# A transformer block on one Trainium2 core: the first attention with its queries turned by DMA and its scores in 2-byte parts

## The reference, cut to what matters

```python
def _L0_xattn_ref(text, features, Wq_w, Wq_b, Wk_w, Wk_b, fn_w, qn_w, kn_w):
    features_n = rmsnorm(features, fn_w)
    Q = einsum('btd,fd->btf', text, Wq_w) + Wq_b
    K = einsum('bsd,fd->bsf', features_n, Wk_w) + Wk_b
    Q = rmsnorm(Q, qn_w)
    K = rmsnorm(K, kn_w)
    scores = einsum('btf,bsf->bts', Q, K) / sqrt(512)
    attn = softmax(scores, axis=-1)
    return einsum('bts,bsf->btf', attn, features_n)
x = x + _L0_xattn_ref(_layernorm(x), ctx_4096, ...)
x = x + _L0_ffn_ref(_layernorm(x), ...)       # sparse feed-forward, inner width 1792
x = x + _L1_xattn_ref(_layernorm(x), ...)     # 32 heads over 8 key heads
x = x + _L1_ffn_ref(_layernorm(x), ...)       # 512 x 512 with a row selection
```

## Time and profile before

| | us |
|---|---|
| median of 3 runs (lowest, highest) | 1484.04 (1482.01, 1485.4) |
| the profiled execution, its own time | 1483.17 |
| its span, first to last instruction | 1481.4 |
| PE busy | 1455.0 (98%) |
| DVE busy | 1120.7 (76%) |
| ACT busy | 792.4 (53%) |
| POOL busy | 713.1 (48%) |
| DMA: moved | 150.04 MB, mean 101 GB/s |

### The profile page before, as it was taken

How to read it: one execution, slowest core, us unless ns; L and a number is a source line. 1 busy time by engine, 2 the same in 40 slices (tenths; PEclk the granted TensorE clock), 3 DMA queues, 4 the chain that set the end, 5 groups by cost and what they waited for, 6 DMA issues and landing times.

```text
span 1481.4 us, 27790 instructions
## 1 busy us (share of the span) xinstructions
PE 1455.0 (98%) x9944; PEld 851.6 (57%) x9944; DVE 1120.7 (76%) x2159; ACT 792.4 (53%) x3201; POOL 713.1 (48%) x672
## 2 busy tenths in 40 slices
PE   8999999999999989999999999999999999999998
PEld 7888645555555455556555555655555565555554
DVE  6887787888876878676776776777677677677868
ACT  6678731211223775565556646654754664565663
POOL 6678885554555354343333434333442433343554
PEclk9999999999999999999999999999999999999999
DMA  5844345444343585534443543444454345233543
GB/s 194 245 143 144 121 93 118 100 85 98 70 82 69 124 164 91 132 84 73 102 93 65 106 77 79 98 89 83 89 90 93 81 82 108 53 63 68 105 70 125
DMA packets 363722, 150.04 MB, mean 101 GB/s; under 512 B 346704, under 2 KB 347344, under 8 KB 360640
## 3 DMA queue, kind: packets, MB, share of 16 engines
q1 hardware_dynamic: 362288, 140.92, 44.4%
q10 hardware_dynamic: 1296, 7.34, 1.5%
HBM read 60.11 MB, written 4.19 MB: 43 GB/s over the span
## 4 chain that ended last, share of the span: by engine, by line
PE 59%; DVE 3%; POOL 1%; ACT 1%; issue 1%; SPq 1%; DMA 0%; POOLq 0%; DVEq 0%; ACTq 0%
PE bank L72 19%; PE bank L74 19%; PE bank L73 19%; PE bank L2667 3%; DVE x_res L2343 1%; ACT a_prob L1986 1%; DVE a_oT_lo L2256 0%; POOL a_xr_lo L1863 0%; DVE a_kn L2211 0%; SPq L1735 0%; DVE a_qve L2195 0%; DVE a_p_lo L2244 0%; POOL w L1902 0%; SPq L1731 0%; ACT xln L124 0%
## 5 line engine op out<-in xcount | busy, mean ns | idle before, releaser
L1986 ACT ACTIVATE a_prob<-a_prob,a_nmx 128x64 f32<-128x64 f32 x512 | 170.2, 334 | 247.7 <-DVE a_nmx L2232 247.7
L1838 POOL TENSOR_TENSOR a_prob<-a_prob,a_mask 128x512 f32<-128x512 f32 x64 | 79.8, 1268 | 271.8 <-DVE a_prob L2226 271.8
L72 PE MATMUL bank<-w,xT_hi 128*128 128x448 f16 (+1 forms) x512 | 187.5, 366 | 1.1 <-PEq L1043 1.1
L74 PE MATMUL bank<-w,xT_hi 128*128 128x448 f16 (+1 forms) x512 | 187.3, 366 | 0.0
L73 PE MATMUL bank<-w,xT_lo 128*128 128x448 f16 (+1 forms) x512 | 187.2, 366 | 0.0
L1856 POOL TENSOR_TENSOR a_qrs<-a_qve,neg_half 128x8 f32<-128x8 f32 x64 | 105.0, 1642 | 138.3 <-DVE a_qve L2195 138.0
L2179 DVE SCALAR_TENSOR_TENSOR x_res<-bank,a_oinv,x_res 128x512 f32<-128x512 f32 x128 | 95.6, 747 | 79.4 <-PE bank L74 79.4
L1251 ACT CAST f_h_hi<-h 128x448 f16<-128x448 f32 x64 | 35.6, 563 | 207.2 <-DVE h L1325 207.2
L2184 DVE SCALAR_TENSOR_TENSOR a_qr_lo<-bank,a_qr_hi 128x512 f16<-128x512 f32 x128 | 87.9, 687 | 45.7 <-ACT a_oT_lo L1963 27.3
L1844 POOL TENSOR_TENSOR a_p_hi<-a_prob,a_rden 128x512 f16<-128x512 f32 x64 | 69.4, 1085 | 104.6 <-DVE a_rden L2240 104.6
L1189 POOL TENSOR_TENSOR f_h_lo<-h,f_h_hi 128x448 f16<-128x448 f32 x64 | 72.7, 1140 | 89.0 <-ACT f_h_hi L1251 89.0
(11 more groups left out here) (357 smaller groups left out, 4443.5 us busy)
## 6 DMA issues: line engine op xcount, KB each, us to landing
shared<-in_l_wq SPq DMA_DIRECT2D x8, 1024.0 KB, 4.9
shared<-in_l_wo SPq DMA_DIRECT2D x8, 1024.0 KB, 5.1
shared<-in_w ACTq DMA_DIRECT2D x8, 896.0 KB, 4.6
craw<-in_w SPq DMA_DIRECT2D x11, 512.0 KB, 3.8
a_wide<-in_l_ctxT SPq DMA_DIRECT2D x16, 256.0 KB, 3.9
x_res<-in_x SPq DMA_DIRECT2D x16, 256.0 KB, 4.5
shared<-in_ctx SPq DMA_DIRECT2D x16, 256.0 KB, 4.3
shared<-in_l_wkv SPq DMA_DIRECT2D x8, 512.0 KB, 3.7
```

Of the source, the lines that this page charges most:

```text
L72: pe.matmul(out, a_hi, b_hi, start=first, stop=False)
L74: return pe.matmul(out, a_hi, b_lo, start=False, stop=last)
L1838: pool.tensor_tensor(blocks(prob[u][:, :]), blocks(prob[u][:, :]), mask[:, :].unsqueeze(1).broadcast_to([P, NB, S]), ALU.add).then_inc(s_m ...
L1986: ins = act.activation(pt, pt, ACT.Exp, bias=nmx[:, col:col + 1], accum_out=den[:, col:col + 1])
```

## The change

Six things change, all in the first attention but for the last:

1. The queries stay unturned in their bank. A 13th matmul adds the bias there (`share`, a matrix of 1/64, times the bias rows split in two parts). DVE no longer adds it. `q_bank(n)` alternates between two banks; the one for PE's turned queries is gone.
2. ACT reads the bank, multiplies by the inverse root of the queries and rounds to f16 (`q_hi`), DVE makes the f16 rest (`q_lo`), and SP turns both parts with a DMA transpose each (`queries_T`, 128 x 512 in 2 bytes).
3. Keys are scaled by a power of two and split in f16; the scores are 12 matmuls of f16.
4. The probabilities of tile n-1 are turned, and the values of n-1 multiplied, in body n, behind the keys and the queries of n+1. On PE the scores and the turn of the keys end the body.
5. ACT, DVE, POOL and the start have new orders, shown below. The queue of SP has two transposes in each round, behind the loads and at n = 4 behind the six small loads, too. The w2 loads 2 to 4 of the next stage come behind the last transposes.
6. In the tail, the first product of the next stage (`hidden(0, 0)`) moves ahead of the last `attend`.

```diff
+    part = lambda n: big[:, 4 * KD * D + n * D:4 * KD * D + (n + 1) * D].rearrange("p (k f) -> p k f", k=KD)
+    xT_hi, xT_lo, cT_hi, cT_lo, bq_parts = (part(n) for n in range(5))
+    qT_hi, qT_lo, kT_hi, kT_lo = (turned[:, n, :, :] for n in range(4))
...
+        def queries_T(n):
+            if n:
+                sp.wait_ge(s_s, n)
+            sp.wait_ge(s_qh, n + 1)
+            sp.dma_start_transpose(qT_hi, qr_hi).then_inc(s_qT, 16)
+            sp.wait_ge(s_ql, n + 1)
+            sp.dma_start_transpose(qT_lo, qr_lo).then_inc(s_qT, 16)
...
+            if n >= 4:
+                queries_T(n - 3)
...
+        first_w2()
+        for n in range(NT - 3, NT):
+            queries_T(n)
@@ pool_steps, body @@
             if first:
                 key_root(1)
+                weigh(1)
             tile_roots(n)
+            if project:
+                features_lo(n + 1)
             if ahead:
                 features_T(n + 2)
-            if first:
-                weigh(1)
...
-            if project:
-                features_lo(n + 1)
             if ahead:
                 weigh(n + 2)
@@ act_steps @@
         def first_body():
+            key_squares(1)
+            features_T(2)
+            features(1)
             normalise(2)
-            key_squares(1)
-            squares_c(2)
-            features_T(2)
-            rows_T(2)
-            k_T(1)
-            exps(0)
-            q_T(1)
-            probs_T(0)
-            query_squares(1)
-            features(1)
+            query_squares(1)
+            rows_T(2)
+            squares_c(2)
+            squares_c(3)
...
+        def q_hi(n):
+            wait_query_root(act, n)
+            if n:
+                act.wait_ge(s_qT, 32 * n)
+            act.activation(qr_hi, q_bank(n)[:, :], ACT.Copy, scale=qrs(n)).then_inc(s_qh, 1)
@@ act_steps, body @@
+            k_T(n)
+            exps(n - 1)
+            q_hi(n)
...
+            if ahead:
+                features_T(n + 2)
+            probs_T(n - 1)
+            if project:
                 key_squares(n + 1)
...
+            act.activation(kT_hi, blk(bkT), ACT.Copy, scale=k_up[:, :]).then_inc(s_kTh, 1)
@@ dve_steps @@
-        def query_bias(n):
-            dve.wait_ge(s_q, n + 1)
-            dve.tensor_tensor(qb[:, :], bq_bank[:, :], bq, ALU.add).then_inc(s_qb, 1)
+        def key_scale():
+            dve.tensor_reduce(k_max[:, :], wqk, AX.X, ALU.max, apply_absolute_value=True).then_inc(wqk_ok, 1)
...
+        def q_lo(n):
+            dve.wait_ge(s_qh, n + 1)
+            dve.scalar_tensor_tensor(qr_lo, q_bank(n)[:, :], qrs(n), qr_hi, ALU.mult, ALU.subtract).then_inc(s_ql, 1)
@@ pe_steps, project_q @@
+            pe.matmul(blk(q_bank(n)), share[:, :], bq_parts, start=False, stop=True).then_inc(s_q, 1)
@@ pe_steps, body @@
             if project and not first:
                 project_k(n + 1)
+            if not first:
+                probs_T(n - 1)
+            if project:
                 project_q(n + 1)
-            pe.wait_ge(s_kTl, n + 1)
             if not first:
+                attend(n - 1)
             if ahead:
                 rows_T(n + 2)
...
+            scores(n)
+            if project:
+                k_T(n + 1)
...
+        def scores(n):
+            pe.wait_ge(s_kTl, n + 1)
+            pe.wait_ge(s_qT, 32 * (n + 1))
@@ pe_steps, tail @@
         def last(n):
+            filler(pe, 2)
+            probs_T(n)
+            filler(pe, 3)
             attend(n)
-            filler(pe, 2)
+            filler(pe, 4)
```

More of the change, by code:

```diff
@@ L211, in l0_attention @@
     wide = sb("wide", [P, 7 * D])
-    xn, cw, kn, qb, kb = (wide[:, n * D:(n + 1) * D] for n in range(5))
+    xn, cw, kn, q_rows, kb = (wide[:, n * D:(n + 1) * D] for n in range(5))
+    qr_hi, qr_lo = (q_rows.bitcast(F16)[:, n * D:(n + 1) * D] for n in range(2))
     cT_raw = [wide[:, n * D:(n + 1) * D].rearrange("p (k f) -> p k f", k=KD) for n in (5, 6)]
@@ L223, in l0_attention @@
     css = lambda n: first_ss[:, n:n + 1] if n < 2 else sums[:, 2:3]
-    qss = sums[:, 3:4]
+    first_qss, first_qrs, share = sb("first_qss", [P, 1]), sb("first_qrs", [P, 1]), sb("share", [P, P], F32R)
+    share_f = kb[:, 0:P]
+    k_max, k_pow, k_inv, k_up, s_down = (sb(n, [P, 1]) for n in ("k_max", "k_pow", "k_inv", "k_up", "s_down"))
+    qss = lambda n: sums[:, 3:4] if n else first_qss[:, :]
     rs = lambda n: first_rs[:, n:n + 1] if n < 3 else root4[:, (n - 3) % RING, 0:1]
@@ L851, in split_wq @@
                 dve.tensor_tensor(w_lo[0][:, k, :], w_raw[0][:, k, :], w_hi[0][:, k, :], ALU.subtract).then_inc(wl_ok, 1)
+        dve.wait_ge(half_ok, 3)
+        dve.tensor_copy(share[:, :], share_f).then_inc(off_ok, 1)
         split_wk((0, 1))
@@ L868, in dve_steps @@
         scale_keys(0)
-        q_T(0)
+        key_scale()
+        rows_T(1)
+        q_lo(0)
+        k_T(0)
         statistics(2)
-        k_T(0).then_inc(s_kTl, 1)
-        rows_T(1)
         run(body)(dve)
+        denominators(NT - 1)
+        probs_T(NT - 1)
         before_last()
@@ L979, in pe_steps @@
         pe.wait_ge(half_ok, 2)
-        project_k(0, first=True)
+        project_k(0, first=True, ks=range(0, 2))
         stay_busy(8)
+        project_k(0, first=True, ks=range(2, 3))
         rows_T(0)
-        stay_busy(10)
+        project_k(0, first=True, ks=range(3, KD))
+        stay_busy(6)
         project_q(0, first=True)
```

321 lines of the change are left out of this document (172 added, 149 removed).

## The result

The changed kernel takes 1503.58 us, the median of four runs (1500.62 to 1505.87), against 1483.94 (1482.01 to 1485.40, four runs). The ratio is 1.0128, with a 95% interval of 1.0114 to 1.0142: 1.3% slower. I had said 1491, and 1479 to 1499 as the range, so the sign was right and the size was not.

What follows compares the result with a forecast made beforehand. PE was taken as busy nearly throughout, with a loop through POOL and DVE next to bind. Start +6.7, body 1 +1.1, bodies 2 to 14 -2.4 and tail +2.6 gave +8.0 us, so 1491, range 1479 to 1499.

Steps and rivals of the forecast that it cites:

- Bounds and sign: Whole kernel: the first attention's end shifts the rest one for one; PE saves 0.8 us a body, almost all lost; slower.
- the sum: Whole kernel: +6.7 + 1.1 - 2.4 + 2.6 = +8.0 us on the profiled 1483.17, giving 1491.2.
- The start, +6.7: Up to tile 2's keys: a chain through ACT, POOL and DVE makes them 6.7 us late, bounds 5 to 8.
- Body 1 and SP's queue, +1.1: Body 1: tile 1's transposes queue on SP behind loads and six small loads, adding 1.1 us, bounds 0 to 3.
- Bodies 2 to 14, -2.4: Bodies 2 to 14 of the first attention: 120.3 us against 122.7, so 2.4 us gained.
- The ring: Bodies 2 to 14: a dependency loop through POOL and DVE, including the search, sets most bodies; 9.7 us in 8 to 12.
- 13.6 us of POOL's waiting: Kernel before, bodies 2 to 14: POOL's idle time for the keys' scaling, read as a loop turning at nearly PE's pace.
- The tail, +2.6: End of the first attention, to the first block score: 2.6 us lost to waits and clock, bounds 1 to 5.
- my 0.9 for it: Tail: the slowed PE clock after longer idling costs 0.9 us, beside 1.75 for waits.
- Behind the attention, 0: Everything after the first attention: merely shifted with its end, no term of its own in the sum.
- The clock: Start and body 1: three longer PE waits would each cost another 1 to 1.75 us by the rule, giving 1496.
- Transposes land late in every body: Rival for the bodies: transposes behind loads on SP cost 0.7 us in each of 13, 9 more, 1500; chance 0.12.

Runs made afterwards that it cites:

- e13: Changed kernel with the w1 pieces searched in the order 2, 3, 0, 1, so that two w1 loads fall away; 1500.86 us.
- e9: Changed kernel in which POOL no longer waits for DVE's scaling of the keys ahead of weigh; 1500.04 us.
- e1: Changed kernel in which POOL, in the first body, splits the turned context of tile 2 right behind weigh(1); 1503.57 us.
- e2: Changed kernel with a new first-body order on POOL and ACT, the split of tile 2's turned context ahead of weigh(1); 1505.27 us.
- e5: Changed kernel with the six small loads issued early, in SP's idle time near 28 us, not ahead of tile 1's transposes; 1498.92 us.
- e14: The bundle with two loads of w1 fewer; 1484.64 us, ratio 0.9998 to the kernel before.
- e7: Changed kernel with DVE's search for the largest weights right behind the scaling of the keys; 1501.45 us.
- e16: The kernel before the change, with POOL not waiting for DVE's scaling of the keys in a body; 1493.86 us against 1485.40.
- the bundle: Changed kernel with small loads early, new POOL and ACT start, tail reordered, POOL's keys wait gone, keys' bias earlier, a w2 piece split in the tail; 1488.30 us.
- e4: Changed kernel with DVE's search for the largest weights at the end of a body, behind the scores; 1502.06 us.

## Why the prediction was wrong, point by point

- **Bounds and sign.** Right: what the attention's end loses is lost one for one, all but 1.8 us, and PE's saving is real (bodies in which PE waits for nothing take 8.11 in e13 and 8.27 in e9; I had 8.15) and is eaten by waits. The profiled execution is 9.4 us over the sum's 1491.2: 1.4 from the start, 1.5 from body 1, 4.1 from bodies 2 to 14, 0.5 from the tail and 1.8 from behind it.
- **The start, +6.7.** The mechanism was there link by link, ending in POOL's L447 as named; it measured 8.1, just above my upper bound of 8. The mis-sized piece is the first: the statistics of tile 2 (DVE, L739) ended at 26.57, not 25.3, and from there the chain took 12.35 where I had 12.2. But as a term of the sum it fails: e1 and e2 brought 3.5 and 6.9 us of it back for nothing, since the DMA behind it was then as late. Of the end of body 1 it was one of two causes, not a length to be added.
- **Body 1 and SP's queue, +1.1.** This is the step that failed first. I counted the small loads as 4.2 us of SP and the transposes at the quiet 2.4 to 2.5 us of the earlier trace rows. SP's part held: the second transpose was issued 7.8 us behind the keys of tile 2, 8.1 in my sum. The landing did not: the scores followed 4.1 behind that issue, not 2.5, and up to 9.0 was measured (e2). The term measured 2.6 in the fastest execution, 4.7 us when the small loads were taken away (e5) and 3 us more in other executions (e13's wait of 5.18 against 2.06).
- **Bodies 2 to 14, -2.4.** The second failed step and the largest, 4.1 us off. The ring is not what failed: the sum had 9.7, 11.0 and 29.1 for bodies 8 to 12, 9.96 on average, and they take 10.12. It exists in the new order (9.35 with POOL's wait gone in e9, 8.93 in e14), but the search is some 0.3 of it (e7), not the 1.1 I charged. What I took for nothing is in the other bodies. Body 2 took 9.44, not 8.65: behind body 1's wait the granted clock was 0.51 until 54.92, which cost some 1.3 us (2.68 for six matmuls, 1.39 for the next six). Body 5 took 9.29, not 8.2, with 1.03 of waiting for transposes. Bodies 13 and 14 took 19.1, not 17.45, and what makes that up I did not isolate. My argument from the earlier trace rows, that 13.6 us of POOL's waiting mean a ring at its limit in the kernel before, is refuted by e16 as a reading of what would help there: the wait at that edge also kept DVE and POOL apart.
- **The tail, +2.6.** 3.1, within its bounds, with the wait named (2.52 ahead of `attend(14)`), but the split was wrong and its sum near by luck. PE's idle time is 14.01 - 9.49 = 4.5 us, and was 10.9 - 9.53 = 1.4, which is all of it. The clock cost as much before (0.84 over 10.9 us) as after (0.88 over 14.01), so my 0.9 for it came to nothing.
- **Behind the attention, 0.** 1.8 us. 1.03 of it is PE's wait at 197.32, which the kernel before and the bundle do not have. The split of w2's pieces on ACT is its likely cause (POOL waits 6.3 us for it, 1.4 before); the bundle, which has one of them earlier, ends 1307.6 behind its first block score, not 1308.1. That is argued, not shown, and the stretch varies: with nothing changed in it, it is 1310.3 in e5.
- **The clock.** The Trainium skill (TensorE: Matmul & The Clock Gate, What's actually happening) has the slow clock as the default and activity as what releases it; by that I had each long wait cost 1 to 1.75 us more, beside the sum and not in it. The last two rows of the windows agree. Behind the 3.03 us wait PE went at 0.50 of its clock, the lower level, and the 12 matmuls took 5.29 us, against 2.85 (56.33 to 59.18) for as many in body 2 at the higher level. That lay ahead of the 2.06 us in which PE waited for the transposes, so most of it cost nothing. Behind that second wait it cost the 1.3 us of body 2. It is not every wait: in e4 PE waited 3.03 us at the scores of tile 1, and the clock from 51.60 to 54.30 was 1.00. The sum with it, 1496, was nearer, but it priced three waits alike, and they cost from nothing to 1.3 us.
- **Rivals.** "Transposes land late in every body" had 0.12 and came nearest in time, 1500. Not in every body: in most they land in 2.4 us, and the longest waits, at the scores of tiles 1 and 5, go when the small loads (e5) or two loads of w1 (e13) do. It should have had more, as a price that varies, and the range reached to 1499 on its account only.

## What to carry to other kernels

The same 128 KB transpose landed in 2.4 to 10.8 us here, by what was ahead of it and beside it: take such a price from a stretch as crowded as the one it moves to, and look at what each queue has in flight there. When two causes end at one instruction, cure both before you call either harmless. An engine's wait in a tuned kernel can be the guard of another engine's speed; take it away alone once before counting on its time. And when a stretch misses its sum, compare body by body before blaming the mechanism: here the ring was right to 0.2 us a body, and the miss lay beside it.
